# Second attention of a four-layer kernel: phases of twelve weight tiles in place of eight, and the intake of the next unit tied to tiles of the first half unit

## The reference, cut to what matters

```python
def _L0_attn_b_ref(X, W_in, b_in, W_out, b_out):      # X is layernorm(x) already
    Xn = (X - mu) / jnp.sqrt(var + LN_EPS)
    P = jnp.einsum('btd,ed->bte', Xn, W_in) + b_in
    P = P.reshape(b, t, h, 4 * dh).transpose(0, 2, 1, 3)      # h = 16 heads, dh = 16
    Q, K, V, G = jnp.split(P, 4, axis=-1)
    sq = q2 + jnp.swapaxes(k2, -1, -2) - 2.0 * jnp.einsum('bhqd,bhkd->bhqk', Q, K)
    dist = jnp.sqrt(jnp.maximum(sq, 0.0))
    W = (SHEP_EPS + dist) ** (-2)
    W = W / (SHEP_EPS + jnp.sum(W, axis=-1, keepdims=True))
    A = jnp.einsum('bhqk,bhkd->bhqd', W, V)
    O = (G * A).transpose(0, 2, 1, 3).reshape(b, t, d)
    return X + jnp.einsum('btd,ed->bte', O, W_out) + b_out
```

## Time and profile before

| | us |
|---|---|
| median of 3 runs | 3925.99 |
| lowest and highest | 3925.09, 3933.21 |
| the profiled execution's own time | 3925.91 |
| its span in the trace | 3923.9 |
| busy in the whole span: TensorE, VectorE, ScalarE, GpSimd | 3503.8, 2509.0, 2223.4, 677.2 |

### The profile page before, as it was taken

How to read it: one execution, slowest core, us unless ns; L and a number is a source line. 1 busy time by engine, 2 the same in 40 slices (tenths; PEclk the granted TensorE clock), 3 DMA queues, 4 the chain that set the end, 5 groups by cost and what they waited for, 6 DMA issues and landing times. The chain is left out here.

```text
span 3923.9 us, 55975 instructions
## 1 busy us (share of the span) xinstructions
PE 3503.8 (89%) x22180; PEld 2472.4 (63%) x22180; DVE 2509.0 (64%) x4349; ACT 2223.4 (57%) x2873; POOL 677.2 (17%) x598
## 2 busy tenths in 40 slices
PE   4999999889999999968778778778867999999998
PEld 3555555478888899963323323323216888889998
DVE  4777777553433455547998998998984443335554
ACT  1666666643322344428998998998983322233443
POOL 3333332100122012121300300300000002200212
PEclk7999999999999999988989889889888999999999
DMA  3000000010010034320000000000001001013342
GB/s 123 1 1 1 1 1 1 1 65 6 28 37 29 35 109 111 101 69 9 1 1 1 1 1 1 1 1 1 1 1 65 6 23 37 24 45 91 93 110 40
DMA packets 86806, 124.93 MB, mean 32 GB/s; under 512 B 7768, under 2 KB 73258, under 8 KB 86545
## 3 DMA queue, kind: packets, MB, share of 16 engines
q1 hardware_dynamic: 68880, 100.18, 7.5%
q0 software_dynamic: 17664, 21.17, 3.2%
HBM read 85.15 MB, written 42.55 MB: 33 GB/s over the span
## 5 line engine op out<-in xcount | busy, mean ns | idle before, releaser
L1830 DVE TENSOR_TENSOR b_w<-b_w 128x2048 f32<-128x2048 f32 x256 | 584.5, 2324 | 24.8 <-ACT b_w L1907 20.8
L1867 ACT ACTIVATE b_w<-b_ring 128x1024 f32<-128x1024 f32 x512 | 485.6, 1039 | 96.9 <-PE b_ring L1949 91.8
L1937 PE MATMUL b_acc<-b_w,b_vg 128*32 128x512 f32 x2048 | 344.5, 754 | 189.8 <-DVE b_w L1830 189.0
L1907 ACT ACTIVATE b_w<-b_w 128x2048 f32<-128x2048 f32 x256 | 468.0, 1897 | 1.4
L1401 ACT ACTIVATE f1hid<-f1ring 128x512 f32<-128x512 f32 (+2 forms) x256 | 132.3, 517 | 577.6 <-PE f1ring L1481 560.6
L1401 ACT ACTIVATE f2hid<-f2ring 128x512 f32<-128x512 f32 (+2 forms) x256 | 132.3, 517 | 576.8 <-PE f2ring L1481 559.7
L1949 PE MATMUL b_ring<-b_qT,b_kT 32*128 32x512 f32 x2048 | 403.8, 683 | 38.9 <-DVE X L1804 23.5
L1319 DVE TENSOR_TENSOR f1hid<-f1hid,f1ring 128x512 f32<-128x512 f32 (+2 forms) x256 | 150.2, 587 | 439.8 <-ACT f1hid L1401 439.7
L1319 DVE TENSOR_TENSOR f2hid<-f2hid,f2ring 128x512 f32<-128x512 f32 (+2 forms) x256 | 150.2, 587 | 439.0 <-ACT f2hid L1401 438.9
L1775 DVE TENSOR_SCALAR b_w<-b_w 128x2048 f32<-128x2048 f32 x256 | 308.6, 1237 | 75.3 <-ACT b_w L1867 74.5
L625 ACT ACTIVATE a_prob<-a_wide 128x1024 f32<-128x1024 f32 (+1 forms) x320 | 292.8, 943 | 82.8 <-PE a_wide L731 56.7
(11 more groups left out here) (337 smaller groups left out, 6237.8 us busy)
## 6 DMA issues: line engine op xcount, KB each, us to landing
X<-expert_in SPq DMA_DIRECT2D x16, 650.0 KB, 5.0
expert_in<-a_zeros SPq DMA_DIRECT2D x8, 650.0 KB, 10.1
X<-in_x SPq DMA_DIRECT2D x4, 1024.0 KB, 10.5
x_mid<-X SPq DMA_DIRECT2D x8, 512.0 KB, 3.1
f1raw_x<-in_rd SPq DMA_DIRECT2D x4, 1024.0 KB
f1raw_xf<-in_rg SPq DMA_DIRECT2D x4, 1024.0 KB, 4.9
f1raw_xf<-in_ru SPq DMA_DIRECT2D x4, 1024.0 KB, 7.0
f1raw_g<-in_rg SPq DMA_DIRECT2D x4, 1024.0 KB, 4.9
```

The lines of the kernel that those rows point to most:

```text
L1830: v.tensor_tensor(one(m), one(m), one(m), ALU.mult).then_inc(s_wts, 1)
L1867: s.activation(w[:, m, 2 * pair:2 * pair + 2, :].rearrange("p h n -> p (h n)"), slot(at + pair), ACT.Ln, scale=SHEP_EPS ** -2).then_inc(R. ...
L1907: s.activation(one(m), one(m), ACT.Sigmoid, scale=-0.5).then_inc(s_sig, 1)
L1937: last = pe.matmul(acc[32 * h:32 * h + 32, qc, :], vg[:, u % 2, h, x, :], w[:, x, h, :], start=(x == 0), stop=(x == TB - 1))
```

## The change

- `w` has twelve places (`RUN = 12`), and tiles are counted through: `g = 8 j + m`, place `g % 12`. A phase is a **run** of twelve tiles: 21 runs of twelve and a last one of four. ScalarE does the sigmoids of a run, then the logs of the next; VectorE the squares of a run, then the bounds of the next.
- On TensorE one dist step of the next run stands ahead of the last values step of a run, and all others behind it.
- The other work is tied to `j` and `m`, wherever the run's borders are. In an even period: qkv ahead of values 1 and 2, take behind squares 2 and 3, squared behind sigmoids 4 and 5, lengths behind squares 5 and 6, stack ahead of values 6 and 7, operand behind squares 6 and 7. In every period: o_rows of the period before behind square 1, back ahead of values 2, gates behind square 3.
- Per batch: moments stays among the bounds, normalise goes behind a square, tokens into the odd period, turn and project one and two tiles away from where they were, add behind square 7; at the very end gates stands ahead of both adds.
- `square` is no buffer of its own any more but lies in half of `xn`, to make room for `w`. The wait of take on `s_gate` is one lower for the first half.

```diff
+    RUN = 12
+    ALL = TB * PERIODS
+    RUNS = [range(g, min(g + RUN, ALL)) for g in range(0, ALL, RUN)]
...
+    def beside(j, m):
+
         b, p = divmod(j, TB)
+        n = j // 2 + 1
+        out = []
+        if j % 2 == 0 and n < UNITS:
+            if m in (1, 2):
+                out += [("qkv", n, m - 1)]
+            if m in (6, 7):
+                out += [("stack", n, m - 6)]
+        if p == 5 and b + 1 < B and m in (5, 6):
+            out += [("tokens", b + 1, m - 5)]
+        if m == 2 and j:
+            out += [("back", j - 1, 0)]
         if p < 2 and b:
-            out += [("turn", b - 1, p), ("project", b - 1, p)]
+            if m == 5:
+                out += [("turn", b - 1, p)]
+            if m == 7:
+                out += [("project", b - 1, p)]
         return out
...
-        for m in range(TB):
-            if m == TB - 4:
-                out += aux + ahead[:1]
-                aux = []
-            elif m > TB - 4:
-                out += ahead[m - TB + 4:m - TB + 5]
-            else:
-                out += aux[:1]
-                aux = aux[1:]
-            out += [("values", j, m)]
-        return out + ahead[4:]
...
+        for run in RUNS:
+            ahead = [d for g in run for d in dist(g + RUN)]
+            for left, g in zip(range(len(run), 0, -1), run):
+                j, m = divmod(g, TB)
+                out += beside(j, m)
+                if left == 1:
+                    out += ahead[:1]
+                    ahead = ahead[1:]
+                out += [("values", j, m)]
+            out += ahead
...
-        w = sb("w", [P, TB, HG, QC])
+        w = sb("w", [P, RUN, HG, QC])
...
+                for run in RUNS:
+                    for g in run:
...
+                        dve.wait_ge(s_sig, g + 1)
+                        v.tensor_tensor(one(g), one(g), one(g), ALU.mult).then_inc(s_wts, 1)
+                        if j % 2 == 0 and n < UNITS:
+                            if m in (5, 6):
+                                lengths(n, m - 5)
+                            if m in (6, 7):
+                                operand(n, m - 6)
+                        if j and m == 1:
+                            o_rows(j - 1)
+                        if j and m == 3:
+                            gates(j - 1)
+                        if j % 2 == 0 and n < UNITS and m in (2, 3):
+                            take(n, m - 2)
+                        if b and p < 2 and m == 7:
                             add(b - 1, p)
...
+                        if p == 5 and b + 1 < B and m == 2:
+                            normalise(b + 1)
+                    for g in run:
+                        if g + RUN < ALL:
+                            bound(g + RUN)
...
+                        act.wait_ge(s_bound, g + 1)
+                        s.activation(one(g), one(g), ACT.Sigmoid, scale=-0.5).then_inc(s_sig, 1)
+                        if p == 5 and b + 1 < B and m in (6, 7):
+                            tokens(b + 1, m - 6)
+                        if j % 2 == 0 and n < UNITS and m in (4, 5):
+                            squared(n, m - 4)
+                        if p < 2 and b and m == 6:
                             turned(b - 1, p)
```

More of the change, by code:

```diff
@@ L1533, in moved, with dist @@
         if p < 2 and b:
-            out += [("turn", b - 1, p), ("project", b - 1, p)]
-        return out
+            if m == 5:
+                out += [("turn", b - 1, p)]
+            if m == 7:
+                out += [("project", b - 1, p)]
+        return out
+    def dist(g):
+        return [("dist", *divmod(g, TB))] if g < ALL else []
     def first():
         out = [("tokens", 0, x) for x in range(2)] + [("qkv", 0, x) for x in range(2)]
-        out += [("stack", 0, i) for i in range(SIDES)]
@@ L1563, in attention_b, with order @@
-    ORDER = [step for j in range(PERIODS + 2) for step in ((first() if j == 0 else []) + order(j))]
+        return out + [("stack", 0, i) for i in range(SIDES)]
+    def order():
+        out = first()
+        for g in RUNS[0]:
+            out += dist(g)
+        for run in RUNS:
[8 more added lines that the diff above has]
+            out += ahead
+        out += [("back", PERIODS - 1, 0)]
+        for x in range(2):
+            out += [("turn", B - 1, x), ("project", B - 1, x)]
+        return out
@@ L1564, in attention_b @@
+    ORDER = order()
     USES = {"dist": 2, "values": 0}
@@ L1770, in operand, with bound @@
                     dve.drain().then_inc(s_qkT, 1)
-                def bound(j, m):
-                    R.wait_free(dve, AT["dist", j, m] + PAIRS - 1 + SLOTS, ())
-                    v.tensor_scalar(one(m), one(m), LOG_MIN, None, ALU.max).then_inc(s_bound, 1)
+                def bound(g):
+                    R.wait_free(dve, AT["dist", *divmod(g, TB)] + PAIRS - 1 + SLOTS, ())
+                    v.tensor_scalar(one(g), one(g), LOG_MIN, None, ALU.max).then_inc(s_bound, 1)
+                    j, m = divmod(g, TB)
+                    b, p = divmod(j, TB)
+                    if b + 1 < B and p == 4 and m == 3:
+                        moments(b + 1)
                 def o_rows(j):
@@ L1820, in _ @@
                     operand(0, i)
-                for m in range(TB):
-                    bound(0, m)
-                for j in range(PERIODS):
-                    b, p = divmod(j, TB)
-                    if j:
-                        gates(j - 1)
-                    n = j // 2 + 1
-                    for m in range(TB):
-                        dve.wait_ge(s_sig, TB * j + m + 1)
-                        v.tensor_tensor(one(m), one(m), one(m), ALU.mult).then_inc(s_wts, 1)
-                        if n < UNITS:
-                            if j % 2 == 0:
-                                if m < 2:
-                                    take(n, m)
-                                if m in (4, 5):
-                                    lengths(n, m - 4)
-                            elif m < SIDES:
-                                operand(n, m)
-                        if b and p < 2 and m == 6:
-                            add(b - 1, p)
-                    for m in range(TB if j + 1 < PERIODS else 0):
-                        bound(j + 1, m)
-                        if m == 3:
-                            o_rows(j)
-                        if b + 1 < B and m == 3:
-                            if p == 1:
-                                moments(b + 1)
-                            if p == 3:
-                                normalise(b + 1)
@@ L1850, in _ @@
                 o_rows(PERIODS - 1)
-                add(B - 1, 0)
                 gates(PERIODS - 1)
-                add(B - 1, 1)
+                for x in range(2):
+                    add(B - 1, x)
                 dve.drain()
```

70 lines of the change are left out of this document (27 added, 43 removed).

## The result

The kernel after takes 4151.41 us (median; 4150.51 to 4152.29), the kernel before 3925.54 in the same runs: a ratio of 1.0582, 95% interval 1.057 to 1.0595, or 226 us more. The forecast was 4193 in a range of 4130 to 4250, slower: right in sign and in range, 42 us too high.

The account below looks back on a forecast made before the run. VectorE and ScalarE, each busy over 90% of the second attention, bound the kernel through their overlap. Terms -32 + 191 - 26 + 50 + 84 + 3 - 2.5 gave +267 us on 3926: 4193 us, range 4130 to 4250.

Parts of the forecast that it names:

- 1 heads: From table load to first square on VectorE, 3.23 us each: ten fewer phases save 32.3 us.
- 2 and 3 exposed logs and turns: Phase ends: logs not covered by squares, +191 us; fewer gaps between last square and last logs, -26 us.
- 7 end: Very end of the attention: gates ahead of both adds lets the transpose follow the first project at once, -2.5 us.
- Rival (a): Fewer table switches decide: ScalarE's logs never held up, heads and turns won, -58 us, 3868 us; chance 0.04.
- Rival (d): Logs still run under squares, gains and losses cancel near 3926 us; chance 0.02.
- (b): Intake costs almost nothing as TensorE's clock stays high: 48 us or less, turns at lower bound, 4140 us; chance 0.18.
- Step 5: Intake of a unit: VectorE newly waits for qkv, back and the stack's transposes, 15 times, +84 us (48 to 120).
- Step 6: Change of batch: normalise between squares, adds waiting for project, 51 us against 48 before, +3 us.
- Step 4: Back end of a half unit: o_rows copy and gates now stand between VectorE's squares, on the path, +50 us.

Follow-up runs that it names:

- e5: The kernel after with both qkv products one tile earlier on TensorE; 4107.57 us, 1.0465 of the kernel before.
- e6: The kernel after with one extra unused VectorE sum behind the first square of each period; 4166.91 us, 1.0624 of the kernel before.
- e3: The kernel after with phases of eight tiles in place of twelve (RUN = 8); 4184.5 us, 1.0659 of the kernel before.
- e4: The kernel before with one dist step in place of four ahead of a period's last values step; 4065.35 us, 1.0357 of the kernel before.
- e10: e5 with take, squared, lengths, o_rows, back and gates one tile earlier and up to four dist steps in the tail; 4054.29 us, 1.0334 of the kernel before.

## Why the prediction was right, and where it was off

| step | forecast | measured |
|---|---|---|
| 1 heads | -32.3 | -32.4 |
| 2 and 3 exposed logs and turns | +165 | +151 (tails +143.4, first logs +7.3) |
| 4 to 6 back end, intake, batches | +137 | +111 (120.0 less four squares) |
| 7 end | -2.5 | -7.6 |
| the stages around | 0 | +4 |

**Right**: the mechanism and its order of size. There are 22 sigmoid table loads; full phases lie 60.1 to 71.9 apart, 65.6 on average, against 60 to 70; ScalarE idles 8.3 to 14.6 us ahead of its logs in 18 of 21 phases, released by dist, and 0.1 to 6.3 in the other three; VectorE's waits ahead of take, gates and the stack's copy are 1.0 to 3.1 us each; the shares fell to 0.77 and 0.73, against 0.75. Rival (a) fell: the heads brought their 32 us, but ScalarE's logs were held up. Rival (d) is out. (b), a cheap intake at 4140, is nearer to the time than my forecast, but its mechanism is not what happened: the intake waits 64.5 us, on the path (e5), about halfway between its 48 and my 84, and the clock fell in the whole stretch, from 0.87 to 0.83. It leaned on the earlier trace rows for a clock that falls while only values run; the clock fell at 2274.3, when TensorE had been idle since 2271.3.

**Off**, term by term. Step 5, the intake: 84 forecast, 18.9 + 19.0 + 26.6 = 64.5 measured. I took one wait per piece for each of 15 units. Gates waited 13 times, 1.46 each in place of 1.8, with back at full clock (0.60 us, granted 1.00); take waited in 9 units, by 1.0 to 3.1; the stack's copy in all 15, but 2.06 only in ten and 1.19, the figure of the earlier trace rows, in the other five. Step 6: each add was priced with a wait of 3 us, and the six have 5.0 in all, since project had mostly run by then. Step 4 and the rest of 6 leave 111 - 64.5 - 5.0 = 42 us for o_rows, gates and normalise, priced at 50 and 8. That this is less than their length fits e6; their own price was not measured alone.

Steps 2 and 3 came out 14 us too high, and here part of the agreement is luck. I counted 8 bare logs per period before and 22 per phase after, and the turns on top. Eight logs under squares per period was a misreading of the earlier trace rows: in most periods before only five or six of 16 start ahead of the last square's end, so 10 or 11 are bare. In after 24 are, because the values of the last tile but one hold TensorE until the last square is nearly done. Both turns are shorter than I had them or filled with logs, so that the two miscounts nearly cancel: an ordinary tail is 10.7 us before (I had 10.5) and 23.4 after (23.7). What was off is where side work meets the tails. Before, the six periods at a change of batch have tails of 14.4 to 14.9 us, with 2 or 3 logs of 16 under squares; I had charged the full 10.5 here, and the rest to the batches in step 6. After, five phases that have the second qkv near their end have tails of 27.5 to 27.8.

Step 7 left out that project's products would run at full clock: 3.72 each against 5.53 and 5.41 before.

**Not seen**: that the length of the phase and the order of dist are separate. I put 191 us down to phases of twelve with the new order together; e3 and e4 show that the order alone costs 141 with phases of eight, and twelve then give 33 back.

What stays open: a kernel with phases of twelve, four dist steps, and intake and back end placed as before wasn't tried, so it is not shown that it would be slower than before; e10, the nearest, is 3.3% slower.

## What to carry to other kernels

When two engines are each over 90% busy on alternating kinds of work, as here, their overlap is the asset. Before lengthening phases to save switches, price the stretch at each phase's end in which only one of them has work (here 24 logs of 0.93 us) against what a switch costs (here 1.28 us, and nothing where the engine waits anyway). And take such a change apart: here the longer phase helped, and what came with it cost 260 us. Side work belongs where the engine waits for its partner, not between the instructions that its partner waits for. In a list that an engine takes as written, a step moved earlier helps only until it stands ahead of something that another engine needs sooner and shares slots with it.

## What the hardware showed unasked

The same work ahead of the attention ended up to 13 us apart in different kernels' traces (first load at 1793.9 to 1806.7 with phases of eight, 1799.5 to 1810.0 with twelve), so a few us of difference in one stage should be read from that stage. It need not be the kernels: executions of the kernel before alone lie between 3913.6 and 3936.3 us. And added work can pay for part of itself: 35 us of extra sums on VectorE moved the time by 16 to 22, since VectorE waited 12 us less behind them.
